# The line buffers of the first scan: four images side by side, or interleaved

## The chip, the cores and the metric

The kernel runs on one core of a Trainium2 chip. The core's engines each follow their own queue: TensorE (matmuls, with the weight loads beside them), VectorE, ScalarE, GpSimd and SyncE, which issues most DMAs; they meet at semaphores. The metric is the time of the whole kernel on the device, in microseconds (us). Three runs of the kernel before the change took 2135.49, 2137.81 and 2139.49 us, a median of 2137.81.

## The reference

The input x has 4 images of 64 channels of 128 x 128 pixels, in float32. Two blocks follow, each with a spatial mixer and a mixture of experts. The second block's spatial mixer is the part that matters here: four passes over the normalised image, down, up, to the right and to the left. In each, a line of the image depends on the line before it, for all lines in turn:

```
def step(carry, xi):                       # carry: the line before, xi: this line
    y = xi + relu(conv1d(carry, w))        # 9 taps along the line, 64 -> 64 channels, pad 4
    return y, y
_, ys = scan(step, xs[0], xs[1:])
```

So each pass is a chain of 127 convolutions over one line of 128 pixels, for four images at once, and a line can't begin before the line before it is complete.

## The kernel before

The kernel runs its stages one after the other: the wavelet mixer of block 0 (`wavelet_mixer`), the choice of tokens for its experts (`expert_choice`), then `apply_and_first_scan`, the stage of the change, three further passes (`scan_pass`, lines L1150 to L1314) and the second mixture (`top2_mixture`).

*How a line lies in memory.* A line of 128 pixels and 64 channels is folded: the even and the odd pixels stand on two halves of the 128 partitions, so that a line of one image is 64 columns. The 9 taps become `ND = 5` matmuls with a 128 x 128 weight block each, which read the same 64 columns at the column offsets d = 0 to 4. All lines of all images lie in `X`, seen as `Xl` (L950) with the axes slot, image, row, column: one image takes 64 x 64 float32 words of a partition in a slot, and two consecutive lines are in the two slots.

*The line buffers.* `g.yh` and `g.yl` hold the line just computed, with a margin of two columns on both sides: 68 columns for each image (L1807). The convolution is done in a one-pass matmul type (float32r), and to keep float32's precision the line is split: `yh` is the line rounded to that type, `yl` what is left. The taps are split the same way into `Thi` and `Tlo`. `convolve(n)` (L999) runs 15 matmuls of 256 columns into one PSUM bank: five taps of Tlo on yh, five of Thi on yh, five of Thi on yl. It waits for `hi` before the first and for `lo` before the eleventh (L1001, L1006).

*VectorE's part of a line*, `scan_line(n)` (L1104): when the 15 matmuls are done (`conv`), L1115 computes relu(conv) + x and writes it to yh (semaphore `hi`); L1117 computes the same once more and writes it to X as the result, in float32 (`full`); L1101 subtracts yh from it and writes yl (`lo`). All three have 256 elements on 128 partitions. Line 0 is a copy (L1108).

*What else runs in the stage.* In the same loop, written out by hand, the chunks that the scan will read are prepared, in steps t of four lines (i = 0 to 3), two chunks a step. TensorE's order (L1040 to L1057): `convolve`, then for i = 0 the matmuls of `delta` (L1018), for i = 1 `centre` (L1028), for i = 2 `variance` (L1037, L1038), for i = 3 `variance` and `centre`. VectorE's order (L1132 to L1147): `scan_line`, then for i = 0 and 1 `add_delta` (L1123), for i = 2 and 3 `norm` (L1129), which waits for ScalarE's rstd. ScalarE squares the centred chunk (L1066, L1068) and makes rstd (L1072, L1074), GpSimd splits the squares (L1092), SyncE loads the chunks and stores them. The scan stays `BEHIND = 11` lines behind, and its last lines have nothing beside them but the turning of the next pass's taps (L643, L652).

*Other lines that the prediction reads.* L773 and L778 are reductions in `expert_choice`: L773 over consecutive words, L778 over the same number of elements with 64 words from one to the next. L561 in `wavelet_mixer` reads and writes every second word. L1255 copies the first line of a pass to its buffer; in the second of the three later passes, at 1085 us, that line is a column of the image, with 64 words from one element to the next. L1350 copies a block of 128 consecutive words. L1208 is the convolution of the later passes.

Of the kernel before, what the change touches and what calls it, by code (L numbers as in the profile page):

```python
# [22 lines left out]
F32 = mybir.dt.float32  # L23
F32R = mybir.dt.float32r
# [3 lines left out]
ALU = mybir.AluOpType  # L28
AXX = mybir.AxisListType.X

P = 128
B, C, H, W = 4, 64, 128, 128
# [896 lines left out]
def apply_and_first_scan(nc, g, a):  # L929
# [6 lines left out]
    with ExitStack() as ctx:  # L936
# [7 lines left out]
        ps = [m.ps(f"ps{r}") for r in range(2)]  # L944
        xin, x2_out = g.xin, m.sems("x2o", B)
        s = {n: m.sem(n) for n in ("delta", "x2", "centred", "squared", "var", "lnv", "rstd", "normed")}
# [3 lines left out]
        Xl = g.X[:].rearrange("p (s b j w) -> p s b j w", s=2, b=B, j=HP)  # L950
# [3 lines left out]
        inner = slice(2, 2 + 64)  # L954
# [24 lines left out]
        with nc.Block() as block:  # L979
# [16 lines left out]

            @block.tensor
            def _(pe):
                def convolve(n):  # L999
                    out = ps[n % 2][:, 0:B * 64].rearrange("p (b w) -> p b w", b=B)  # L1000
                    pe.wait_ge(s["hi"], n)  # L1001
                    for t in (g.Tlo, g.Thi):
                        for d in range(ND):
                            pe.matmul(out, t[:, d * P:d * P + P], g.yh[:, :, d:d + 64],  # L1004
                                      start=(t is g.Tlo and d == 0), stop=False)
                    pe.wait_ge(s["lo"], n)  # L1006
                    for d in range(ND):
                        last = pe.matmul(out, g.Thi[:, d * P:d * P + P], g.yl[:, :, d:d + 64],  # L1008
                                         start=False, stop=(d == ND - 1))
                    last.then_inc(s["conv"], 1)  # L1010

                def delta(n):
                    k, p = divmod(n // 2, 2)
                    at = p * (TOK + PAD) + k * N
                    wait(pe, s["x2"], n)
                    wait(pe, s["lnv"], n - 1)
                    for i in range(2):
                        last = pe.matmul(dl[i][:], g.D[i * C:i * C + C, p], g.E[i * C:i * C + C, at:at + N],  # L1018
                                         start=True, stop=True)
                    last.then_inc(s["delta"], 2)  # L1020

                def centre(n):
                    wait(pe, s["x2"], n + 1)
                    wait(pe, s["normed"], n - 1)
                    src = buf(n).rearrange("p (q v) -> p v q", v=2)
                    for h, v in ((0, 0), (1, 1), (0, 1), (1, 0)):
                        rows = slice(h * C, h * C + C)
                        last = pe.matmul(xc[n % 2][v * C:v * C + C, h], g.Cm[rows, rows], src[rows, v],  # L1028
                                         start=True, stop=True)
                    last.then_inc(s["centred"], 1)  # L1030

                def variance(n):
                    wait(pe, s["parts"], n + 1)
                    wait(pe, s["high"], n + 1)
                    wait(pe, s["lnv"], n)
                    wait(pe, s["x2"], min(n // 2 * 2 + (4 if n % 2 else 2), CHUNKS))
                    pe.matmul(vv[:], Jr[:], sq_hi[n % 2][:], start=True, stop=False)  # L1037
                    pe.matmul(vv[:], Jr[:], sq_lo[n % 2][:], start=False, stop=True).then_inc(s["var"], 1)  # L1038

                for t in range(STEPS):  # L1040
                    for i in range(4):
                        n = line(t, i)
                        if n is not None and n >= 1:
                            convolve(n)
                        if i == 0 and t < PAIRS:
                            delta(2 * t)
                        if i == 1 and t < PAIRS:
                            centre(2 * t)
                        if i == 2 and 1 <= t <= PAIRS:
                            variance(2 * t - 1)  # L1050
                        if i == 3 and t < PAIRS:
                            variance(2 * t)
                            centre(2 * t + 1)
                        if n == FREE:
                            pe.wait_ge(s["normed"], CHUNKS - 1)
                            pe.wait_ge(g.unit_ready, 1)
                            turn_taps(pe, g, 1, wn, unit, banks[0])  # L1057
# [37 lines left out]
            @block.vector  # L1095
            def _(dve):
                def split(x, n):

                    wait(dve, s["full"], n)
                    dve.wait_ge(s["hi"], n + 1)  # L1100
                    dve.tensor_tensor(g.yl[:, :, inner], x, g.yh[:, :, inner].bitcast(F32), ALU.subtract  # L1101
                                      ).then_inc(s["lo"], 1)

                def scan_line(n):  # L1104
                    x = Xl[:, n % 2, :, n // 2:n // 2 + 1, :].rearrange("p b j w -> p b (j w)")
                    if n == 0:
                        wait(dve, s["normed"], B)
                        dve.tensor_copy(g.yh[:, :, inner], x).then_inc(s["hi"], 1)  # L1108
                        split(x, 0)
                        return  # L1110
                    conv = ps[n % 2][:, 0:B * 64].rearrange("p (b w) -> p b w", b=B)
                    dve.wait_ge(s["conv"], n)
                    if n % (2 * JR) == 0:
                        wait(dve, s["normed"], (n // (2 * JR) + 1) * B)
                    dve.scalar_tensor_tensor(g.yh[:, :, inner], conv, 0.0, x, ALU.max, ALU.add  # L1115
                                             ).then_inc(s["hi"], 1)
                    dve.scalar_tensor_tensor(x, conv, 0.0, x, ALU.max, ALU.add).then_inc(s["full"], 1)  # L1117
                    split(x, n)

                def add_delta(n):  # L1120
                    dve.wait_ge(s["delta"], n + 1)
                    dve.wait_ge(xin[n % B], n // B * 16 + 16)
                    dve.tensor_tensor(buf(n), dl[n % 2][:], buf(n), ALU.add).then_inc(s["x2"], 1)  # L1123

                def norm(n):
                    k, b = divmod(n, B)
                    at = b * HP * WP + k * (JR * WP)
                    dve.wait_ge(s["rstd"], n + 1)
                    dve.tensor_tensor(Xv[:, :, at:at + JR * WP], xc[n % 2], halves(sq(n)), ALU.mult  # L1129
                                      ).then_inc(s["normed"], 1)  # L1130

                for t in range(STEPS):  # L1132
                    for i in range(4):
                        n = line(t, i)
                        if n is not None:
                            scan_line(n)
                            if n == FREE - 4:
                                dve.wait_ge(s["delta"], CHUNKS - 2)
                                dve.tensor_tensor(unit, g.Cm[0:C, 0:C], g.J[0:C, 0:C], ALU.add).then_inc(g.unit_ready, 1)
                            if FREE + 3 <= n < FREE + 7:  # L1140
                                copy_taps(dve, g, 1, banks[0], n - FREE - 3)
                        if i < 2 and t < PAIRS:
                            add_delta(2 * t + i)
                        if i == 2 and 1 <= t <= PAIRS:
                            norm(2 * t - 1)
                        if i == 3 and t < PAIRS:
                            norm(2 * t)  # L1147
# [614 lines left out]
def metaformer_kernel(nc, a, out):  # L1762
    g = Shared()
    with ExitStack() as ctx:
# [30 lines left out]
        with ExitStack() as early:  # L1795
            me = Mem(nc, early, "g")
            g.E = me.sb("E", [P, 2 * TOK + PAD])
            g.T = {}
            with ExitStack() as choice:
                mc = Mem(nc, choice, "g")  # L1800
                g.cand = mc.right("cand", [P, B // 2, NG * K0])
                choice_constants(g)
                setup_block0(nc, g, a)
                wavelet_mixer(nc, g, a)
                g.D = me.sb("D", [P, B // 2, P])
                g.Thi, g.Tlo = me.sb("Thi", [P, ND * P], F32R), me.sb("Tlo", [P, ND * P], F32R)
                g.yh, g.yl = me.sb("yh", [P, B, 68], F32R), me.sb("yl", [P, B, 68], F32R)  # L1807
                expert_choice(nc, g, a)
            second = ctx.enter_context(ExitStack())
            g.T[1] = Mem(nc, second, "g").right("T1", [P, ND * P])  # L1810
            apply_and_first_scan(nc, g, a)
# [38 lines left out]
```

## Time and profile before

| | |
|---|---|
| Median of 3 runs | 2137.81 us (2135.49 to 2139.49) |
| Profiled execution | span 2135.2 us, 40582 instructions; the page gives no other time for it |
| TensorE busy | 2023.2 us (95%) |
| VectorE busy | 1193.0 us (56%) |
| First scan's convolutions | 1905 matmuls, 429.4 to 791.5 us |
| L1004 on Tlo, mean of one | 306 ns, 635 of them |
| L1004 on Thi, mean of one | 285 ns, 635 |
| L1008, mean of one | 288 ns, 635 |
| L1115, mean of one | 426 ns, 127 |
| L1101, mean of one | 449 ns, 128 |

The span runs from the first to the last instruction of one profiled execution. A busy TensorE isn't TensorE at its peak: its matmuls overlap, and a matmul's duration holds the filling and emptying of the array, so what one costs in a row is the step from its start to the next one's. The granted clock is the share of full speed that TensorE was given.

### The profile page before, as it was taken

The page shows a single profiled execution, that of the slowest core. Times are in us where ns is not written, and L with a number is a line of the kernel's source. Part 1 is how long each engine was busy: PE and PEld are TensorE (multiplying, and loading weights), DVE is VectorE, ACT ScalarE, POOL GpSimd, SP SyncE. Part 2 cuts the span into 40 slices and gives each one's busy share as a digit, 9 for nine tenths or more (in the row PEclk, how much of TensorE's full clock was granted, in tenths as well). Part 3 has the DMA queues.
Part 4 walks back from the last instruction along what each step waited for, and adds up shares of the span by engine and source line. Part 5 has one row for each costly group of instructions (what it writes and reads, how often), then busy time and mean ns, then how long its engine had stood idle before and what let it go on. Part 6 is the DMA issues. An engine that isn't in the chain of part 4 may idle for free. (4 is left out here: it accounts for less than half of the span.)

```text
span 2135.2 us, 40582 instructions
## 1 busy us (share of the span) xinstructions
PE 2023.2 (95%) x14414; PEld 1528.4 (72%) x14414; DVE 1193.0 (56%) x2548; ACT 1005.2 (47%) x2815; POOL 511.6 (24%) x622
## 2 busy tenths in 40 slices
PE   6999992699999989999999999999999799999998
PEld 3555551377777779999999999999999444444443
DVE  5777778666666653222222222232222599999998
ACT  4666664334444423333344444444444545455452
POOL 4555543222222210000000000000000554555541
PEclk9999996599999999999999999999999799999999
DMA  4955541223223210000000000000000466655653
GB/s 117 242 164 169 163 144 50 68 87 99 90 90 99 86 36 1 0 0 0 0 4 0 0 0 0 20 0 0 0 0 0 114 153 149 153 151 149 153 137 90
DMA packets 192672, 159.04 MB, mean 74 GB/s; under 512 B 25848, under 2 KB 159000, under 8 KB 192536
## 3 DMA queue, kind: packets, MB, share of 16 engines
q1 hardware_dynamic: 190840, 156.89, 26.4%
q8 instruction: 61, 1.00, 0.2%
q0 software_dynamic: 512, 0.53, 0.1%
q14 instruction: 75, 0.61, 0.1%
q10 hardware_dynamic: 1184, 0.00, 0.0%
HBM read 56.70 MB, written 67.11 MB: 58 GB/s over the span
## 5 line engine op out<-in xcount | busy, mean ns | idle before, releaser
L1208 PE MATMUL s_ps<-g_ring,g_T 128*128 128x128 f32 x7620 | 855.7, 274 | 8.5 <-DVE g_ring L1255 8.5
L1208 PEld LDWEIGHTS s_ps<-g_ring,g_T 128*128 128x128 f32 x7620 | 854.6, 192 | 9.2 <-DVE g_ring L1255 9.1
L1244 DVE SCALAR_TENSOR_TENSOR g_ring<-s_ps,s_xs 128x128 f32<-128x128 f32 x508 | 148.7, 293 | 418.3 <-PE s_ps L1208 418.3
L1685 DVE TENSOR_TENSOR tm_Z<-tm_pg,tm_nd 128x1024 f32<-128x1024 f32 x256 | 301.9, 1211 | 22.9 <-PE tm_pg L1525 22.5
L1307 ACT ACTIVATE g_X<-g_ring 128x256 f32<-128x256 f32 x254 | 172.3, 678 | 296.0 <-DVE g_ring L1244 296.0
L1539 PE MATMUL tm_po<-tm_Z,g_wexp 128*64 128x512 f32 x1024 | 249.2, 608 | 0.0
L1291 ACT ACTIVATE g_X<-g_ring 64x256 f32 x256 | 106.9, 418 | 205.5 <-DVE g_ring L1244 203.3
L1244 DVE SCALAR_TENSOR_TENSOR g_ring<-s_ps,g_X 128x128 f32<-128x128 f32 x254 | 74.4, 293 | 210.6 <-PE s_ps L1208 210.6
L1621 POOL TENSOR_TENSOR g_X<-g_x,g_X 128x512 f32<-128x512 f32 x64 | 82.9, 1298 | 349.7 <-POOLq L1184 286.0
L1302 ACT ACTIVATE s_xs<-g_X 128x256 f32<-128x256 f32 x254 | 161.3, 636 | 0.6 <-PEq L1184 0.6
L1539 PEld LDWEIGHTS tm_po<-tm_Z,g_wexp 128*64 128x64 f32 x1024 | 62.5, 137 | 109.9 <-issue 108.1
L1330 POOL MEMSET g_zero<- 128x1 f32 x1 | 0.1, 98 | 578.2 <-POOLq L1184 578.2
L1598 ACT ACTIVATE tm_gT<-tm_bankB 64x512 fp32r<-64x512 f32 x64 | 37.8, 591 | 202.0 <-PE tm_bankB L1513 202.0
L1004 PEld LDWEIGHTS af_ps<-g_yh,g_Tlo 128*128 128x128 f32 x635 | 85.0, 190 | 66.8 <-DVE g_yh L1115 54.3
L533 POOL TENSOR_TENSOR wm_sql<-g_X,wm_sqh 128x512 fp32r<-128x512 f32 x64 | 89.1, 1393 | 132.9 <-DVE wm_sqh L568 131.6
L1004 PE MATMUL af_ps<-g_yh,g_Tlo 128*128 128x256 f32 x635 | 111.5, 306 | 5.9 <-DVE g_yh L1115 4.2
L1115 DVE SCALAR_TENSOR_TENSOR g_yh<-af_ps,g_X 128x256 fp32r<-128x256 f32 x127 | 54.1, 426 | 90.4 <-PE af_ps L1008 87.7
L1008 PE MATMUL af_ps<-g_yl,g_Thi 128*128 128x256 f32 x635 | 99.2, 288 | 0.0
L1004 PE MATMUL af_ps<-g_yh,g_Thi 128*128 128x256 f32 x635 | 98.0, 285 | 0.0
L1525 PE MATMUL tm_pg<-tm_gT,g_sel 32*128 32x512 f32 x512 | 96.2, 449 | 1.2 <-DVE tm_Z L1685 1.1
L1008 PEld LDWEIGHTS af_ps<-g_yl,g_Thi 128*128 128x128 f32 x635 | 86.6, 192 | 0.0
L1004 PEld LDWEIGHTS af_ps<-g_yh,g_Thi 128*128 128x128 f32 x635 | 86.1, 190 | 0.0
(273 smaller groups left out, 2887.7 us busy)
## 6 DMA issues: line engine op xcount, KB each, us to landing
tm_nd<-g_X SPq DMA_DIRECT2D x256, 128.0 KB, 2.4
g_X<-in_x SPq DMA_DIRECT2D x128, 128.0 KB, 2.9
x1s<-g_X SPq DMA_DIRECT2D x64, 256.0 KB, 2.1
x1tok<-g_X SPq DMA_DIRECT2D x64, 256.0 KB, 2.5
g_x<-x2s SPq DMA_DIRECT2D x64, 256.0 KB, 2.9
y<-tm_yo SPq DMA_DIRECT2D x128, 128.0 KB, 2.5
g_X<-x1s SPq DMA_DIRECT2D x32, 256.0 KB, 2.8
x2s<-g_X SPq DMA_DIRECT2D x32, 256.0 KB, 2.0
```

Source lines behind the costliest of these rows:

```text
L533: pool.tensor_tensor(sq_lo[:], sq[c % 2], sq_hi[:].bitcast(F32), ALU.subtract).then_inc(s["parts"], 1)
L1004: pe.matmul(out, t[:, d * P:d * P + P], g.yh[:, :, d:d + 64], start=(t is g.Tlo and d == 0), stop=False)
L1008: last = pe.matmul(out, g.Thi[:, d * P:d * P + P], g.yl[:, :, d:d + 64], start=False, stop=(d == ND - 1))
L1208: last = pe.matmul(out, g.T[i][:, d * P:d * P + P], g.ring[(u - 1) % RING][:, images(c), d:d + 64], start=(d == 0), stop=(d == ND - 1))
L1244: dve.scalar_tensor_tensor(g.ring[n % RING][:, images(c), inner], conv, 0.0, x[:, images(c)], ALU.max, ALU.add).then_inc(y_ready[c], 1)
L1291: last = act.activation(dst.rearrange("p b j w -> p b (j w)"), src, ACT.Copy)
L1302: act.activation(xs[n % RING][:], line(*place(n)), ACT.Copy).then_inc(staged, 1)
L1307: act.activation(line(*place(n)), g.ring[n % RING][:, :, inner], ACT.Copy).then_inc(stored, 1)
L1525: last = pe.matmul(pg[q % 2][:, h * N:h * N + N], sel[rows, at:at + 2].rearrange("p e c -> p (e c)"), gT[i][rows], start=True, stop=True)
L1539: last = pe.matmul(po[i][h * C:h * C + C, :], wexp[:, ep], Z[q % 4][:, h], start=False, stop=(ep == EP - 1), skip_group_check=True)
L1621: pool.tensor_tensor(xv, natural(x2[t % 2][i][:]), xv, ALU.add).then_inc(s["x3"], 1)
L1685: dve.tensor_tensor(Z[q % 4][:], pg[q % 2][:].rearrange("p (h n) -> p h n", h=2), nd[t % 2][i][:], ALU.mult).then_inc(s["z"], 1)
```

## The change

The two buffers get the shape 68 columns by 4 images, instead of 4 images by 68 columns: in a partition the four images' words of one column stand beside each other. The window of a tap, `y[:, d:d + 64, :]`, is then one run of 256 words, where it was four runs of 64 with 68 words from the start of one to that of the next. The columns of the PSUM bank come in the same order, column by column, and VectorE's three operations follow it: they walk `x`, which keeps its place in X, across the images first. So x's elements are taken from four places in turn, one image's 64 x 64 words apart. Number and size of the instructions, semaphores and their waits, and all other stages are unchanged.

```diff
             def _(pe):
+                def window(y, d):
+
+                    return y[:, d:d + 64, :].rearrange("p w b -> p (w b)")
+
                 def convolve(n):
-                    out = ps[n % 2][:, 0:B * 64].rearrange("p (b w) -> p b w", b=B)
+                    out = ps[n % 2][:, 0:B * 64]
                     pe.wait_ge(s["hi"], n)
                     for t in (g.Tlo, g.Thi):
                         for d in range(ND):
-                            pe.matmul(out, t[:, d * P:d * P + P], g.yh[:, :, d:d + 64],
+                            pe.matmul(out, t[:, d * P:d * P + P], window(g.yh, d),
                                       start=(t is g.Tlo and d == 0), stop=False)
                     pe.wait_ge(s["lo"], n)
                     for d in range(ND):
-                        last = pe.matmul(out, g.Thi[:, d * P:d * P + P], g.yl[:, :, d:d + 64],
+                        last = pe.matmul(out, g.Thi[:, d * P:d * P + P], window(g.yl, d),
                                          start=False, stop=(d == ND - 1))
...
-                    dve.tensor_tensor(g.yl[:, :, inner], x, g.yh[:, :, inner].bitcast(F32), ALU.subtract
+                    dve.tensor_tensor(g.yl[:, inner, :], x, g.yh[:, inner, :].bitcast(F32), ALU.subtract
                                       ).then_inc(s["lo"], 1)
...
-                    x = Xl[:, n % 2, :, n // 2:n // 2 + 1, :].rearrange("p b j w -> p b (j w)")
+                    x = Xl[:, n % 2, :, n // 2, :].rearrange("p b w -> p w b")
...
-                        dve.tensor_copy(g.yh[:, :, inner], x).then_inc(s["hi"], 1)
+                        dve.tensor_copy(g.yh[:, inner, :], x).then_inc(s["hi"], 1)
...
-                    conv = ps[n % 2][:, 0:B * 64].rearrange("p (b w) -> p b w", b=B)
+                    conv = ps[n % 2][:, 0:B * 64].rearrange("p (w b) -> p w b", b=B)
...
-                    dve.scalar_tensor_tensor(g.yh[:, :, inner], conv, 0.0, x, ALU.max, ALU.add
+                    dve.scalar_tensor_tensor(g.yh[:, inner, :], conv, 0.0, x, ALU.max, ALU.add
                                              ).then_inc(s["hi"], 1)
                     dve.scalar_tensor_tensor(x, conv, 0.0, x, ALU.max, ALU.add).then_inc(s["full"], 1)
...
-                g.yh, g.yl = me.sb("yh", [P, B, 68], F32R), me.sb("yl", [P, B, 68], F32R)
+                g.yh, g.yl = me.sb("yh", [P, 68, B], F32R), me.sb("yl", [P, 68, B], F32R)
```

## Rows read from the trace of the kernel before

**Rows 1.** Windows: window, length, then busy time (instructions) of each engine, clock, DMA.

```profile
465.50:751.30 285.80, 284.39 (x2105) 218.49 (x2101) 185.42 (x401) 117.47 (x201) 64.10 (x50) 1.00 0.29 93
```

**Rows 2.** Timeline, one turn of four lines: start, duration, engine, line, operation, idle before.

```profile
602.69 0.88 PE L1004 MATMUL af_ps<-g_yh,g_Tlo 128*128 128x256 f32 x5
...
604.83 0.43 DVE L1115 SCALAR_TENSOR_TENSOR g_yh<-af_ps,g_X 128x256 fp32r<-128x256 f32 x1 [0.56 <-PE af_ps L1008]
...
605.78 0.88 PE L1004 MATMUL af_ps<-g_yh,g_Tlo 128*128 128x256 f32 x5
606.07 0.68 DVE L1123 TENSOR_TENSOR g_E<-af_dl,g_E 128x512 f32<-128x512 f32 x1
...
607.81 0.68 PE L1028 MATMUL af_xc<-g_E,g_Cm 64*64 64x256 f32 x8
607.92 0.43 DVE L1115 SCALAR_TENSOR_TENSOR g_yh<-af_ps,g_X 128x256 fp32r<-128x256 f32 x1 [1.17 <-PE af_ps L1008]
...
608.42 0.87 PE L1004 MATMUL af_ps<-g_yh,g_Tlo 128*128 128x256 f32 x5
...
608.71 0.43 DVE L1101 TENSOR_TENSOR g_yl<-g_X,g_yh 128x256 fp32r<-128x256 f32 x1
...
609.62 0.68 PEld L1008 LDWEIGHTS af_ps<-g_yl,g_Thi 128*128 128x128 f32 x5
...
609.73 0.78 PE L1008 MATMUL af_ps<-g_yl,g_Thi 128*128 128x256 f32 x5
...
610.35 0.39 PE L1037 MATMUL af_dl<-af_sqh,g_J 128*128 128x512 f32 x1
...
611.03 0.87 PE L1004 MATMUL af_ps<-g_yh,g_Tlo 128*128 128x256 f32 x5
...
612.39 0.69 DVE L1129 TENSOR_TENSOR g_X<-af_xc,g_E 128x512 f32<-128x512 f32 x1 [0.63 <-ACT g_E L1074]
...
614.13 0.88 PE L1004 MATMUL af_ps<-g_yh,g_Tlo 128*128 128x256 f32 x5
```

**Rows 3.** Timeline of the stage's tail, one weight load of a line.

```profile
778.99 0.67 PEld L1004 LDWEIGHTS af_ps<-g_yh,g_Tlo 128*128 128x128 f32 x5 [0.72 <-DVE g_yh L1115]
```

**Rows 4.** Source lines, one line's Thi and yl matmuls: duration min/median/max, first and last start.

```profile
L1004 PE MATMUL af_ps<-g_yh,g_Thi x2: 283/284/286, 603.4 to 603.5; 128*128 128x256 f32 x2
...
L1004 PE MATMUL af_ps<-g_yh,g_Thi x2: 284/287/290, 603.6 to 603.8; 128*128 128x256 f32 x2
...
L1004 PE MATMUL af_ps<-g_yh,g_Thi x1: 277/277/277, 603.9 to 603.9; 128*128 128x256 f32 x1
...
L1008 PE MATMUL af_ps<-g_yl,g_Thi x1: 282/282/282, 604.0 to 604.0; 128*128 128x256 f32 x1
...
L1008 PE MATMUL af_ps<-g_yl,g_Thi x2: 292/292/292, 604.1 to 604.3; 128*128 128x256 f32 x2
...
L1008 PE MATMUL af_ps<-g_yl,g_Thi x2: 279/284/289, 604.4 to 604.5; 128*128 128x256 f32 x2
```

**Rows 5.** Source line of the variance matmul; timeline of TensorE in a later pass.

```profile
L1037 PE MATMUL af_dl<-af_sqh,g_J x64: 390/390/797, 410.1 to 770.5; 128*128 128x512 f32 x64
...
899.76 6.41 PE L1208 MATMUL s_ps<-g_ring,g_T 128*128 128x128 f32 x56
```

**Rows 6.** Source line L1115, whole stage.

```profile
L1115 DVE SCALAR_TENSOR_TENSOR g_yh<-af_ps,g_X x127: 424/426/426, 433.0 to 791.5; 128x256 fp32r<-128x256 f32 x127
```

**Rows 7.** Source lines of other VectorE operations, in order or hopping.

```profile
L773 DVE TENSOR_REDUCE g_X<-g_X x1: 1221/1221/1221, 373.7 to 373.7; 128x16 f32<-128x1024 f32 x1
...
L778 DVE TENSOR_REDUCE g_X<-g_X x1: 1872/1872/1872, 377.2 to 377.2; 128x128 f32<-128x1024 f32 x1
...
L561 DVE SCALAR_TENSOR_TENSOR g_X<-wm_rec,g_b2c,g_X x128: 473/482/490, 28.9 to 327.6; 128x256 f32<-128x256 f32 x128
...
L1255 DVE COPY g_ring<-g_X x2: 339/340/342, 1085.2 to 1085.5; 128x128 f32<-128x128 f32 x2
...
L1350 DVE COPY g_rx<-g_Cm x1: 217/217/217, 1394.4 to 1394.4; 128x128 f32<-128x128 f32 x1
```

## The prediction

> **What bounds the kernel now.** I read the windows by stage first, then the timeline of one turn of the four-step loop, then the tail of the stage, and last the single instructions. The change touches only the stage of the first scan. Between 465.5 and 751.3 us TensorE is busy for 284.4 of 285.8 us at a granted clock of 1.00, its upper level of 2.4 GHz, and VectorE for 185.4 [rows 1]. TensorE's busy time holds pipeline tails, so the timeline has to say what ends last. In it four lines start at 602.69, 605.78, 608.42 and 611.03 and the next turn at 614.13: 3.09, 2.64, 2.61 and 3.10 us, 11.44 us a turn, and so over the whole stage [rows 2]. There are two kinds of gap between lines:
>
> - *Serial.* Line 608.42 starts when its g_yh is there: L1115 starts at 607.92, takes 426 ns, and the convolution follows within 0.1 us [rows 2, 6]. There a line is convolution, L1115, convolution, and the centre or variance matmuls between are shorter than the gap. The gaps behind the second and the third line of a turn are such (29 turns, 58 gaps); in the tail, where TensorE has nothing else and waits 0.72 us for g_yh, there are 9 more [rows 3]: 67.
> - *Covered.* L1115 of line 605.78 starts at 604.83 and ends at 605.26, but TensorE is still at its delta matmuls until the line starts at 605.78. L1115 has 0.47 us to spare here, if the 0.05 that a serial gap also needs is taken off [rows 2]. The gap behind the fourth line (variance, then centre) is like it: 59 in all.
>
> **Part 1: the columns of a tap (a gain).** A line is 15 matmuls, five taps for each of Tlo and Thi on yh and Thi on yl. The five yl matmuls from 609.73 to 610.35 take 124 ns a step [rows 2] and last 282, 292, 292, 289 and 279 ns, 287 in the mean [rows 4]: a step is the duration less 163. The Thi group lasts 283 and 286, then 284 and 290, then 277. So the middle taps are the slow ones. The diff fits this: today a tap's window starts 4 bytes after the last one's, in four runs of 64 columns, so only the first and the last tap start at a multiple of 16 bytes of the row; after it every window is one run and starts at such a multiple. The trace has one contiguous stream of this type, the variance matmul, 390 ns for 512 columns [rows 5]; against 277 for 256 that is 0.44 ns a column, 113 for 256, and 113 is also the step of a matmul that lasts 277. So I take 277 for all. The excess is 35 ns in Thi, 49 in yl, and 29 in Tlo (taken like Thi's last four, since its first only fills the pipeline): 113 ns a line. TensorE is on the path in both kinds of gap, so 127 x 113 = **14.4 us less**. Bounds: nothing (the columns are not what costs), and the 112 ns at which a weight load of this shape and a matmul alternate in the later passes (56 in 6.41 us, [rows 5]), 14 steps x 2.4 more: 147 ns a line, 18.7 us.
>
> **Part 2: VectorE's three operations a line (a loss).** L1115, L1117 and L1101 keep their 256 elements, but walk x across the images, so each element of x lies 16 KB (one image's 64 x 64 words) from the one before. L1115 and L1101 read one such stream; L1117 reads it and writes it. The trace has no such hop. The nearest rows [rows 7]: a reduction of 1024 elements takes 1221 ns in order and 1872 with hops of 64 words, 0.64 ns an element, 163 for 256; an operation on every second word (L561) takes 482 against L1115's 426, 56 more; a copy of 128 elements with hops of 64 words takes 340 against 217 in order, 123 more, 245 for 256, though a plain copy may lose more by it than these do. I take 163, the row with the long hopping stream and nothing else; 56 and 245 are the ends. A gain is excluded: no element is saved.
>
> The Trainium skill, "Vector Engine (DVE) Microarchitecture Reference", section 5.2 (measured stream behaviour on trn2), speaks against this change: a port keeps its rate only on runs of two or more adjacent words, and one source that hops at every element costs 1.73 instead of 1.054 ns a column. By it the loss would be 173 ns an operation and the sum 0.7 us higher. This trace's 0.64 ns an element agrees.
>
> On the path: L1115 counts in each serial gap, 67 x 163 = **10.9 us more**. In the 59 covered gaps it lies beside the matmuls, within the 0.47; without that cover it would cost 9.6. L1117 and L1101 lie beside the ten yh matmuls: L1101 ends at 609.14, and the first yl weights load at 609.62, 0.48 us later [rows 2]. The ten yh matmuls get 0.06 shorter, which leaves 0.42. L1101 takes 0.16 of it, L1117 between 0.16 (read and write hop together) and 0.33 (they add up); by the middle the two take 0.41 and are just hidden. Beyond that, each ns late costs 67 serial gaps one. At the end of the stage all three hold up the next: **0.6 us more**.
>
> Queued behind them on VectorE: L1123, which ends at 606.75 and would end 0.57 later, still before the centre matmuls at 607.81 that wait for it [rows 2]. The normalisation L1129 waits for ScalarE until 612.39; L1101 before it, 0.72 us after its line's start as in line 608.42, would end at 612.32. A turn holds 7.4 us of VectorE's work (185.4 of 285.8, [rows 1]) and gains 2.3, of 11.4: it is not the bound as a whole. L1108 runs once, off the path.
>
> **Sum.** -14.4 + 10.9 + 0.6 = -2.9 us. The profiled execution's span is 2135.2 us, 0.3 under the fastest of the three runs and 2.6 under their median, so its durations hold for the median to about a thousandth. 2137.8 - 2.9 = **2134.9 us**.
>
> **The rivals.**
>
> *B, the matmuls gain more.* One run in place of four brings the step to the later passes' 112 ns: 18.7 us instead of 14.4, 2130.6. For it: the four runs go, and not only their offsets. Against: the contiguous 512 columns need 0.44 ns each. The Trainium skill, "TensorE: Matmul & The Clock Gate", section "Back-to-back issue gap", gives N/2.4 + 2.5, 109 ns for 256 columns; by that rule the gain would be some 23 us and the time 2126. The trace's contiguous matmul, 390 ns for 512, speaks against it.
>
> *C, the hop is almost free.* Each image's words are still read in order, four streams in turn, and a hop costs no more than L561's 56 ns: 3.8 us in place of 10.9, 0.2 at the end, 2127.4. For it: L561. Against: the reduction's hops cost three times that. Section 5.2 of the Trainium skill's page on the Vector Engine also reports one stream between two regions 16 KiB apart at the full read rate; no run here shows it.
>
> *D, it doesn't do what it says.* The spread among taps comes from something else, such as the weight loads beside them, and the steps stay: only the loss is left, +11.5, 2149.3. For it: yl's taps last up to 292, Thi's up to 290, and the second is 292 in one and 286 in the other at the same offset. Against: first and last are quick in both.
>
> *E, slower: the low parts come late.* Place: the wait before the first yl matmul; the other yl matmuls and so the next L1115 stand behind it. It decides once L1117 and L1101 lose over 0.42 us together. At 0.2 an operation, double for L1117, they lose 0.6: 67 x 0.18 = 12.1, and L1115 costs 13.4, 0.8 at the end: 2149.7. At 245 and double: 67 x 0.315 = 21.1 and 16.4 and 1.0: 2161.9. For it: the forecast lies at the edge of the room, and L1117 hops on two ports. Against: at 163 and double it is only 0.07 a gap, 4.7 us.
>
> **How the numbers follow.** About 0.2%, 4.3 us, is what a measurement can tell from no change. The forecast has 0.42; 20 ns an operation and 25 ns a line either way, and that 4.7, give it 2130 to 2142, a third of it faster and the rest within. B has 0.14 and C 0.12, both faster; D has 0.08, slower; E has 0.24, 0.04 of it within. Faster 0.40, same 0.32, slower 0.28. The range goes down to where B and C hold together (18.7 less, 3.8 and 0.2 more), 2123, and up past D and E's first price, 2156.
>
> **What would show it.** Part 1: af_ps matmuls all at about 277 ns; if they keep 282 to 292, D. Part 2: L1115 and L1101 at about 590 ns, L1117 between 580 and 740; under 500 is C, over 625 E. The chain: serial lines of 2.66 to 2.69 us, covered ones of 2.98; a wait of TensorE for g_yl is E. The prediction is wrong if a line's time leaves these by over 0.1 us, or if the centre or variance matmuls begin to wait for VectorE.

## The result, and the profile after

The change makes the kernel slower: 2143.04 us (median of 9 runs, 2141.47 to 2145.46) against 2135.49 of the kernel before (9 runs, 2134.58 to 2139.52), a ratio of 1.0032 with a 95% interval of 1.0023 to 1.0041. The forecast was 2134.9, 2.9 us faster than the median then known; the range from 2123 to 2156 holds the result, but the sign is wrong.

| | before | after |
|---|---|---|
| Profiled span | 2135.2 us | 2143.6 us |
| yl matmul, median | 289 ns | 280 ns |
| Operation on the path (L1115, now L1119), median | 426 ns | 604 ns |
| Start of the first to start of the last low-part operation (L1101, now L1105) | 428.1 to 792.3, 364.2 us | 429.8 to 799.6, 369.8 us |

Three source lines of the kernel before, from which the table and the differences below are taken (duration ns min/median/max, first and last start):

```profile
L1008 PE MATMUL af_ps<-g_yl,g_Thi x635: 276/289/416, 431.7 to 791.2; 128*128 128x256 f32 x159
...
L1117 DVE SCALAR_TENSOR_TENSOR g_X<-af_ps,g_X x127: 412/414/424, 433.3 to 791.9; 128x256 f32<-128x256 f32 x127
...
L1101 DVE TENSOR_TENSOR g_yl<-g_X,g_yh x128: 425/427/531, 428.1 to 792.3; 128x256 fp32r<-128x256 f32 x128
```

The line numbers behind the diff are four higher: L1004 and L1008 are now L1008 and L1012; L1101, L1115 and L1117 are L1105, L1119 and L1121. Now the single instructions, one source line each, which answer to [rows 4, 6]:

```profile
L1008 PE MATMUL af_ps<-g_yh,g_Tlo x635: 275/282/581, 430.9 to 796.9; 128*128 128x256 f32 x159
...
L1008 PE MATMUL af_ps<-g_yh,g_Thi x635: 276/281/415, 432.2 to 797.5; 128*128 128x256 f32 x159
...
L1012 PE MATMUL af_ps<-g_yl,g_Thi x635: 274/280/415, 433.2 to 798.1; 128*128 128x256 f32 x159
...
L1119 DVE SCALAR_TENSOR_TENSOR g_yh<-af_ps,g_X x127: 582/604/616, 434.5 to 798.4; 128x256 fp32r<-128x256 f32 x127
...
L1121 DVE SCALAR_TENSOR_TENSOR g_X<-af_ps,g_X x127: 585/605/621, 435.1 to 798.9; 128x256 f32<-128x256 f32 x127
...
L1105 DVE TENSOR_TENSOR g_yl<-g_X,g_yh x128: 587/629/642, 429.8 to 799.6; 128x256 fp32r<-128x256 f32 x128
```

Both halves of the change are in these rows. The groups of taps no longer differ: the median is 280 to 282 ns in all three, where taps 1 to 3 stood at up to 292. And each of VectorE's operations is longer by 178 to 202 ns. One turn of four lines, the timeline that answers to [rows 2]:

```profile
606.55 0.86 PE L1008 MATMUL af_ps<-g_yh,g_Tlo 128*128 128x256 f32 x5
...
609.57 0.86 PE L1008 MATMUL af_ps<-g_yh,g_Tlo 128*128 128x256 f32 x5
...
611.65 0.61 DVE L1119 SCALAR_TENSOR_TENSOR g_yh<-af_ps,g_X 128x256 fp32r<-128x256 f32 x1 [0.67 <-PE af_ps L1012]
...
612.32 0.86 PE L1008 MATMUL af_ps<-g_yh,g_Tlo 128*128 128x256 f32 x5
...
612.82 0.62 DVE L1105 TENSOR_TENSOR g_yl<-g_X,g_yh 128x256 fp32r<-128x256 f32 x1
...
613.50 0.66 PEld L1012 LDWEIGHTS af_ps<-g_yl,g_Thi 128*128 128x128 f32 x5
...
615.06 0.86 PE L1008 MATMUL af_ps<-g_yh,g_Tlo 128*128 128x256 f32 x5 [0.18 <-DVE g_yh L1119]
...
618.12 0.38 PE L1008 MATMUL af_ps<-g_yh,g_Tlo 128*128 128x256 f32 x1
```

The lines start at 606.55, 609.57, 612.32 and 615.06, the next turn at 618.12: 3.02, 2.75, 2.74 and 3.06 us, where they took 3.09, 2.64, 2.61 and 3.10. The covered gaps got 0.04 to 0.07 us shorter, the serial ones 0.11 to 0.13 longer. In a serial gap L1119 starts at 611.65, ends at 612.26, and the line starts at 612.32. L1105 of this line ends at 613.44, and the weights for yl load at 613.50, as soon behind it as the line starts behind L1119. So the load waits for the low part. In some lines one sees what it costs, as in this one of the tail:

```profile
777.84 0.64 DVE L1105 TENSOR_TENSOR g_yl<-g_X,g_yh 128x256 fp32r<-128x256 f32 x1
...
777.90 0.66 PEld L1008 LDWEIGHTS af_ps<-g_yh,g_Thi 128*128 128x128 f32 x5
...
778.53 0.65 PEld L1012 LDWEIGHTS af_ps<-g_yl,g_Thi 128*128 128x128 f32 x5
```

The low part ends at 778.48, the yl loads begin 0.05 us later, and the five loads before them took 0.63 us, where those of line 609.57, in a covered gap, take 0.60 (610.15 to 610.75). The single loads in the trace give the sum. In some 66 lines the first yl load starts 52 to 62 ns behind the low part's end, and in the others 325 ns or more. In the 66 it comes 134 ns behind the load before it in the mean, in the others 116: 18 ns late, 1.2 us in all. No wait is listed for it in the profile, since the load before it is still running. In the tail TensorE's wait for g_yh grows from 0.72 us [rows 3] to 0.88:

```profile
785.50 0.66 PEld L1008 LDWEIGHTS af_ps<-g_yh,g_Tlo 128*128 128x128 f32 x5 [0.88 <-DVE g_yh L1119]
```

The window of the stage's middle (busy time of each engine, clock, DMA) has TensorE at the upper clock, as [rows 1] had; VectorE is busy for 237.5 of 286.0 us, where it was for 185.4 of 285.8.

```profile
470.00:756.00 286.00, 279.60 (x2076) 213.10 (x2073) 237.52 (x396) 115.32 (x196) 63.69 (x50) 1.00 0.28 93
```

*Where the 8.5 us between the two spans lie.* The stage grew by 5.6 us. Another 1.7 us came before it: L778 starts at 378.8 and not 377.2, in code that is unchanged, and it does so in some kernels below and not in others (378.9 in the first experiment, 377.2 in the third), so it isn't the change's. The last 1.2 us lies behind the stage's end, 1.0 of it in the next pass. The two windows of 16 us there, before and after, each from shortly ahead of the last split:

```profile
790.00:806.00 16.00, 13.13 (x102) 12.93 (x101) 5.02 (x24) 3.34 (x8) 1.20 (x2) 0.89 0.14 38
```

```profile
796.00:812.00 16.00, 12.27 (x83) 12.07 (x84) 6.27 (x24) 1.71 (x5) 1.20 (x2) 0.79 0.14 38
```

The granted clock is 0.89 in the one and 0.79 in the other: after the break between the stages it was at its lower level for longer. This too varies from run to run: among the runs of the kernel before that were taken beside experiment 4, the mean granted clock is 0.969 to 0.973. The ratio's interval, 4.9 to 8.8 us, holds the stage's 5.6.

### The profile page after: what moved, and what is told of

It is laid out like the page before. It is cut to its first block and busy times, and to the rows that moved or that the text cites. A ratio compares the mean times of both kernels' runs of the same rounds, so it can differ in the third digit from the quotient of the medians.

```text
span 2143.6 us, 40582 instructions
## 1 busy us (share of the span) xinstructions
PE 2021.7 (94%) x14414; PEld 1524.4 (71%) x14414; DVE 1262.1 (59%) x2548; ACT 1006.5 (47%) x2815; POOL 511.8 (24%) x622
## 5 line engine op out<-in xcount | busy, mean ns | idle before, releaser
L1625 POOL TENSOR_TENSOR g_X<-g_x,g_X 128x512 f32<-128x512 f32 x64 | 83.0, 1299 | 349.6 <-POOLq L1188 286.0
L1008 PEld LDWEIGHTS af_ps<-g_yh,g_Tlo 128*128 128x128 f32 x635 | 83.5, 189 | 76.1 <-DVE g_yh L1119 75.3
L1008 PE MATMUL af_ps<-g_yh,g_Tlo 128*128 128x256 f32 x635 | 109.7, 303 | 13.1 <-DVE g_yh L1119 10.3
L1119 DVE SCALAR_TENSOR_TENSOR g_yh<-af_ps,g_X 128x256 fp32r<-128x256 f32 x127 | 76.5, 603 | 58.5 <-PE af_ps L1012 55.3
L1012 PE MATMUL af_ps<-g_yl,g_Thi 128*128 128x256 f32 x635 | 96.6, 282 | 0.0
L1008 PE MATMUL af_ps<-g_yh,g_Thi 128*128 128x256 f32 x635 | 96.4, 282 | 0.0
L1008 PEld LDWEIGHTS af_ps<-g_yh,g_Thi 128*128 128x128 f32 x635 | 85.1, 189 | 0.0
L538 POOL TENSOR_TENSOR wm_xl<-g_X,wm_xh 128x512 fp32r<-128x512 f32 x64 | 81.7, 1276 | 13.6 <-DVE wm_xh L555 13.6
```

The costliest lines, as they stand in the source:

```text
L1008: pe.matmul(out, t[:, d * P:d * P + P], window(g.yh, d), start=(t is g.Tlo and d == 0), stop=False)
L1012: last = pe.matmul(out, g.Thi[:, d * P:d * P + P], window(g.yl, d), start=False, stop=(d == ND - 1))
```

## The experiments

Their theories: the first is that the tidy windows were worth some 50 ns a line from the outset, because a matmul with its own weight load can't go much faster, and that the hop costs what it costs on the serial gaps; the main rival is that VectorE's hops took half of the matmuls' gain. Ratios are to the kernel before on the same chip; lengths of the stage are taken as in the table, from the rows of the low-part operation.

**1. The columns alone.** Interleaved buffers, but VectorE reads 256 consecutive words of X and writes its result to 256 others (four rows of one image each, in place of one row of four images).

```diff
-                    x = Xl[:, n % 2, :, n // 2, :].rearrange("p b w -> p w b")
+                    def flat(n, b):
...
+                        return Xl[:, n % 2, b, n // 8 * 4:n // 8 * 4 + 4, :].rearrange("p j w -> p (j w)").rearrange("p (w b) -> p w b", b=B)
...
+                    x, y = flat(n, 0), flat(n, 1)
...
-                    dve.scalar_tensor_tensor(x, conv, 0.0, x, ALU.max, ALU.add).then_inc(s["full"], 1)
...
+                    dve.scalar_tensor_tensor(y, conv, 0.0, x, ALU.max, ALU.add).then_inc(s["full"], 1)
+                    split(y, n)
```

> The interleaved buffers with none of VectorE's hops: its three operations read and write runs of 256 words of x (other rows than the reference's). Theory 1 (a matmul of 256 columns with its own weight load has a floor near 118 ns a step, so the tidy windows were never worth more than some 50 ns a line): the af_ps matmuls stay at 280 ns as in the changed kernel, serial lines are 2.56 to 2.59 us, the kernel 6 to 7 us faster than before (2129 if before is 2135.5). Rival (VectorE's hops take read bandwidth from the matmuls and ate half of the gain): the matmuls drop to 277 ns or less, steps of 114, and the kernel is 13 to 15 us faster than before.

Measured: 2128.25 us, ratio 0.9958 (0.9945 to 0.9972). The source lines:

```profile
L1008 PE MATMUL af_ps<-g_yh,g_Thi x635: 275/281/416, 432.3 to 785.3; 128*128 128x256 f32 x159
...
L1012 PE MATMUL af_ps<-g_yl,g_Thi x635: 274/280/416, 433.4 to 785.9; 128*128 128x256 f32 x159
...
L1123 DVE SCALAR_TENSOR_TENSOR g_yh<-af_ps,g_X x127: 424/425/426, 434.7 to 786.2; 128x256 fp32r<-128x256 f32 x127
...
L1105 DVE TENSOR_TENSOR g_yl<-g_X,g_yh x128: 424/426/595, 429.8 to 787.0; 128x256 fp32r<-128x256 f32 x128
```

And from its timeline, two lines' first matmuls with a serial gap between them:

```profile
604.04 0.86 PE L1008 MATMUL af_ps<-g_yh,g_Tlo 128*128 128x256 f32 x5
...
606.63 0.62 PE L1008 MATMUL af_ps<-g_yh,g_Tlo 128*128 128x256 f32 x3
```

Without any hop the matmuls still last 280 to 281 ns. So VectorE's hops didn't lengthen the matmuls of the changed kernel: the rival falls. The columns are worth 7.0 us of the stage (429.8 to 787.0, 357.2), half of the predicted 14.4. The serial line between 604.04 and 606.63 takes 2.59 us. The median fell by 9.0. The profile's 8.8 are the stage's 7.0, 1.7 more ahead of it, and 3.5 less behind it, where this run's clock didn't fall at a break (granted clock 1.00 from 787 to 803 us). So 7.0, and not 9.0, is the columns' share.

**2. The hop alone.** The old buffers and windows; x is walked across the images.

```diff
...
+                def line_of(y):
...
+                    return y[:, :, inner].rearrange("p a (c b) -> p a c b", b=B)
...
-                    x = Xl[:, n % 2, :, n // 2:n // 2 + 1, :].rearrange("p b j w -> p b (j w)")
+                    x = Xl[:, n % 2, :, n // 2, :].rearrange("p b (a c) -> p a c b", c=16)
...
-                    dve.scalar_tensor_tensor(g.yh[:, :, inner], conv, 0.0, x, ALU.max, ALU.add
+                    dve.scalar_tensor_tensor(line_of(g.yh), conv, 0.0, x, ALU.max, ALU.add
```

> The old buffers and windows, with only the hop across the images in VectorE's three reads and one write of x (the elements are wired wrongly within a line). Theory 1: the matmuls stay as before (282 to 292 by tap, a convolution of 2.10 us), L1115's 426 becomes about 600, serial lines grow by 0.18 us, covered ones by nothing: 67 x 0.178 = 12 us slower than before (2147). Rival (hops also slow the matmuls): convolutions over 2.12 us, 15 us slower or more.

Measured: 2150.84 us, ratio 1.0061 (1.0047 to 1.0074).

```profile
L1008 PE MATMUL af_ps<-g_yl,g_Thi x635: 276/289/415, 432.8 to 803.5; 128*128 128x256 f32 x159
...
L1119 DVE SCALAR_TENSOR_TENSOR g_yh<-af_ps,g_X x127: 584/606/615, 434.1 to 803.9; 128x256 fp32r<-128x256 f32 x127
...
L1101 DVE TENSOR_TENSOR g_yl<-g_X,g_yh x128: 587/622/637, 429.3 to 805.0; 128x256 fp32r<-128x256 f32 x128
```

The matmuls are those of before (yl median 289), L1119 takes 606, and the stage 375.7 us, 11.5 more. The two halves together, -7.0 and +11.5, make +4.5 of the +5.6 that the whole change costs in the stage. The 1.1 us that are left show up only where both halves meet: the quicker matmuls reach the yl taps sooner, and the hops make the low part later. From its first to its last start a line's convolution takes 1768 ns in the changed kernel and 1760 in experiment 1 (means from the traces), 1.0 us over 127 lines; most of this is the late low part of the section above. No run takes that wait alone away.

**3. The hop off the path.** The changed kernel, but L1119 (here L1120) adds consecutive words of a weight tile in place of x.

```diff
+                    other = g.Thi[:, 0:B * 64].bitcast(F32).rearrange("p (w b) -> p w b", b=B)
...
-                    dve.scalar_tensor_tensor(g.yh[:, inner, :], conv, 0.0, x, ALU.max, ALU.add
+                    dve.scalar_tensor_tensor(g.yh[:, inner, :], conv, 0.0, other, ALU.max, ALU.add
```

> The changed kernel, but the operation on the path (L1119) adds 256 consecutive words of another tile in place of x; the two beside the matmuls still hop. Theory 1: what lies beside the yh matmuls costs nothing, so this is as fast as the kernel without any hop, 6 to 7 us under before, with the low part still ready 0.1 us or more before TensorE wants it. Rival (the low parts come late, or the longer VectorE queue holds up others): 3 us or more slower than the kernel without hops.

Measured: 2131.92 us, ratio 0.9976 (0.9966 to 0.9986).

```profile
L1120 DVE SCALAR_TENSOR_TENSOR g_yh<-af_ps,g_Thi x127: 424/425/426, 433.0 to 784.8; 128x256 fp32r<-128x256 f32 x127
...
L1122 DVE SCALAR_TENSOR_TENSOR g_X<-af_ps,g_X x127: 581/606/615, 433.3 to 785.1; 128x256 f32<-128x256 f32 x127
...
L1105 DVE TENSOR_TENSOR g_yl<-g_X,g_yh x128: 590/627/642, 428.2 to 785.7; 128x256 fp32r<-128x256 f32 x128
```

The two operations beside the matmuls hop for 606 and 627 ns, and the stage takes 357.5 us against 357.2 without any hop. What lies beside the yh matmuls is hidden all but for 0.3 us, so rival E of the prediction is no large term. (Here too the first yl load comes late, in 36 lines by 10 ns in the mean.) The medians differ by 3.7 us between these two kernels, with intervals that overlap; the profiles put no more than 0.3 of it into the stage.

**4. All taps at offset 0, old layout.** Four runs of 64 columns, each from a multiple of 16 bytes of its row.

```diff
-                            pe.matmul(out, t[:, d * P:d * P + P], g.yh[:, :, d:d + 64],
+                            pe.matmul(out, t[:, d * P:d * P + P], g.yh[:, :, 0:64],
...
-                        last = pe.matmul(out, g.Thi[:, d * P:d * P + P], g.yl[:, :, d:d + 64],
+                        last = pe.matmul(out, g.Thi[:, d * P:d * P + P], g.yl[:, :, 0:64],
```

> The kernel before with the windows of all five taps at column offset 0 (so the taps' shifts are left out): four runs of 64 columns, each starting on a multiple of 16 bytes. Theory 1 (the offset within 16 bytes made taps 1 to 3 slow, the number of runs costs nothing): all af_ps matmuls at 277 to 283 ns, a convolution near 2.04 us, about 6 us faster than before. Rival (it is the four runs, or the position of the tap in its group): durations keep spreading up to 292 by position, and the time stays within 2 us of before.

Measured: 2130.89 us, ratio 0.9972 (0.9961 to 0.9983).

```profile
L1004 PE MATMUL af_ps<-g_yh,g_Thi x635: 276/281/415, 432.0 to 784.3; 128*128 128x256 f32 x159
...
L1008 PE MATMUL af_ps<-g_yl,g_Thi x635: 277/283/291, 432.8 to 784.9; 128*128 128x256 f32 x159
...
L1101 DVE TENSOR_TENSOR g_yl<-g_X,g_yh x128: 425/427/578, 429.6 to 786.0; 128x256 fp32r<-128x256 f32 x128
```

With the four runs kept and only the offsets gone, the matmuls are as quick as in the new layout and the stage is as short as in experiment 1 (356.4 us against 357.2; in its first 6 us the granted clock was 0.79 here and 0.56 there, an estimate of 1.4 us at full speed, more than the difference). It was the offset, not the number of runs; one run in place of four gave nothing by itself. All five taps read the same columns here; the new layout's windows differ and are as quick, so that doesn't explain it.

**5. The new layout one word off.**

```diff
...
-                g.yh, g.yl = me.sb("yh", [P, 68, B], F32R), me.sb("yl", [P, 68, B], F32R)
+                g.yh_all, g.yl_all = me.sb("yh", [P, 68 * B + 4], F32R), me.sb("yl", [P, 68 * B + 4], F32R)
+                g.yh, g.yl = (t[:, 1:1 + 68 * B].rearrange("p (w b) -> p w b", b=B) for t in (g.yh_all, g.yl_all))
```

> The changed kernel with both line buffers moved by one word, so that every window is one run that starts 4 bytes after a multiple of 16. If a run that starts off costs a fixed bit per run, one run in place of four costs a quarter of it: matmuls at 280 to 283 ns, at most 2 us slower than the changed kernel (2143 to 2145). If the offset slows the whole stream, the matmuls go to 288 to 292 ns, a convolution is 2.10 us again, and the time is 6 us over the changed kernel (2149). VectorE's operations, now writing runs off by a word, may take a little more.

Measured: 2146.08 us, ratio 1.0040 (1.0026 to 1.0054), against 1.0032 for the changed kernel, each on its own chip: no difference that the intervals allow.

```profile
L1008 PE MATMUL af_ps<-g_yh,g_Thi x635: 277/283/416, 431.0 to 800.0; 128*128 128x256 f32 x159
...
L1012 PE MATMUL af_ps<-g_yl,g_Thi x635: 277/284/416, 432.1 to 800.6; 128*128 128x256 f32 x159
...
L1105 DVE TENSOR_TENSOR g_yl<-g_X,g_yh x128: 591/633/641, 428.7 to 802.0; 128x256 fp32r<-128x256 f32 x128
```

The medians are 283 and 284 where the changed kernel has 281 and 280, and the yl taps of the old layout up to 292; the stage takes 373.3 us, 3.5 more than in the changed kernel. One run that starts off costs less than four, but neither expectation's number is met cleanly.

**6. Half the columns.** 14 of 15 matmuls with 128 columns, so that half of each line's convolution is left out.

```diff
-                            pe.matmul(out, t[:, d * P:d * P + P], window(g.yh, d),
+                            cols = B * 64 if t is g.Tlo and d == 0 else 128
+                            pe.matmul(out[:, 0:cols], t[:, d * P:d * P + P], window(g.yh, d)[:, 0:cols],
...
```

> The changed kernel with 128 columns instead of 256 in 14 of the 15 matmuls of a line (half of each line's convolution is left out). If the weight load sets the step, steps stay at 107 to 118 ns and a convolution at 1.9 to 2.05 us, the time within 15 us of the changed kernel. If the stream of columns sets it, steps fall to some 60 ns and a convolution to 1.2 us: some 100 us less in the stage, unless VectorE's operations then take over as the bound (about 1.9 us a line), which caps the gain near 80 us.

Measured: 2386.47 us in one run, against 2137.34 of before. Neither expectation. A window in the stage, and one in the next pass of the same run:

```profile
470.00:790.00 320.00, 320.00 (x1385) 247.84 (x1385) 156.49 (x264) 75.70 (x131) 41.92 (x33) 0.50 0.17 55
...
1050.00:1290.00 240.00, 240.00 (x2145) 239.62 (x2144) 65.47 (x221) 88.53 (x212) 0.00 (x0) 1.00 0.00 0
```

In its timeline, the Thi and yl groups of one line:

```profile
600.84 1.27 PE L1009 MATMUL af_ps<-g_yh,g_Thi 128*128 128x128 f32 x5
601.91 1.27 PE L1013 MATMUL af_ps<-g_yl,g_Thi 128*128 128x128 f32 x5
```

The clock was at its lower level, 0.50, in this window, where TensorE never paused in the profile, and on to the stage's end at 1040 us. The number of columns alone is not the reason: the next pass has matmuls of 128 columns with their own weight loads too, and runs at 1.00, 2145 of them in 240 us or 112 ns each. What held the clock down in the stage stays open. The steps can still be read, beside the first line of the changed kernel, which also ran at the lower level:

```profile
432.18 1.27 PE L1008 MATMUL af_ps<-g_yh,g_Thi 128*128 128x256 f32 x5
433.24 1.27 PE L1012 MATMUL af_ps<-g_yl,g_Thi 128*128 128x256 f32 x5
```

Five matmuls take 1.07 us there with 128 columns and 1.06 with 256 (from the Thi row to the yl row). Half the columns save nothing at the same clock: the columns don't set a step of 213 ns, and what is left of the pair is the weight load.

**7. Three quarters of the columns.** The same with 192 for 128 (a quarter of the convolution is left out), to see the load at the upper clock.

> The changed kernel with 192 columns instead of 256 in 14 of the 15 matmuls of a line (a quarter of the line's convolution is left out). With 128 columns the clock stayed at its lower level and every step was 213 ns, the time of a weight load there; what the load allows at the upper level is still open. If the clock stays at 1.00 and the load sets the step, steps are 107 to 112 ns, 0.1 us a line less than with 256 columns. If instead a step is the columns plus some 11 ns, it is near 91 ns and a convolution some 0.37 us shorter. If the clock falls to 0.50 again, steps are 213 once more, and it stays open.

Measured: 2141.36 us in one run, before 2137.98. The middle of the stage ran at 1.00. The window there:

```profile
470.00:760.00 290.00, 284.75 (x2169) 216.09 (x2167) 247.40 (x415) 120.56 (x205) 65.80 (x52) 1.00 0.28 94
```

Two groups of weight loads of one line, from the timeline:

```profile
605.89 0.64 PEld L1009 LDWEIGHTS af_ps<-g_yh,g_Thi 128*128 128x128 f32 x5
606.45 0.64 PEld L1013 LDWEIGHTS af_ps<-g_yl,g_Thi 128*128 128x128 f32 x5
```

And the Thi matmuls of a few lines, by source line:

```profile
L1009 PE MATMUL af_ps<-g_yh,g_Thi x30: 272/274/280, 600.1 to 614.8; 128*128 128x192 f32 x30
```

Five pairs of load and matmul take 0.56 us, 112 ns a step, though 192 columns alone would take a quarter less than 256. So at the upper clock the step is 112 with 192 columns as with the 128 of [rows 5]: the load holds it there. With 256 columns that start well it is 118 (280 to 282 less the 163 of the prediction), and before it was 122 in the mean. The Trainium skill, "TensorE: Matmul & The Clock Gate", section "LDWEIGHTS (loading the stationary operand)", gives columns / 1.2, 107 ns for 128; these 112 lie 5 ns above it. The 109 of its section "Back-to-back issue gap", which the prediction's rival B took for these pairs, is given there for a matmul alone, and for a stream of load and matmul pairs the section says that both set the spacing; with 256 columns the step here stays at 118 in the mean.

The kernel as a whole gained little by it: the yh taps are now so quick that in some 62 lines the first yl load waits for the low part (179 ns behind the load before it, in the other lines 112), and from 760 to 800 us the granted clock was 0.73.

**8. The fetch ahead: a version that beats both.** The changed kernel, complete; ScalarE copies x of the next lines into four interleaved buffers, so that the operation on the path reads consecutive words. In each step of the loop the copy for the next step's line 0 stands ahead of ScalarE's second square, the others behind it. Every eighth line, whose chunk has only just been normalised, still hops.

```diff
+        xi = [m.sb(f"xi{r}", [P, 64, B]) for r in range(4)]
+        staged = m.sem("staged")
...
+                def fetch(t, i):
+                    n = line(t, i)
+                    if n is None or n % 8 == 0:
+                        return
+                    act.wait_ge(s["normed"], (n // 8 + 1) * B)
+                    wait(act, s["full"], n - 4)
+                    act.activation(xi[n % 4][:], across(n), ACT.Copy).then_inc(staged, 1)
...
+                    early = x if n % 8 == 0 else xi[n % 4][:]
+                    if n % 8:
+                        dve.wait_ge(staged, n - n // 8)
+                    dve.scalar_tensor_tensor(g.yh[:, inner, :], conv, 0.0, early, ALU.max, ALU.add
+                    dve.scalar_tensor_tensor(x, conv, 0.0, early, ALU.max, ALU.add).then_inc(s["full"], 1)
```

> The changed kernel with the whole computation: ScalarE copies each line's x into an interleaved buffer of its own a few lines ahead, so that the operation on the path reads consecutive words (every eighth line still hops). Theory 1: the hop leaves the path, the gain of the windows stays: 5 to 7 us faster than before (2129 to 2130.5), serial lines 2.57 us. Rival (ScalarE has no room, its rstd or the fetch itself comes late, or its hopping reads disturb the others): the on-path operation waits for the fetch or the normalisation comes late, and the time is at or above before's 2135.5.

Measured: 2131.45 us, ratio 0.9972 (0.9962 to 0.9983): about 6 us faster than the kernel before.

```profile
L1140 DVE SCALAR_TENSOR_TENSOR g_yh<-af_ps,af_xi x112: 424/425/426, 433.8 to 785.4; 128x256 fp32r<-128x256 f32 x112
L1140 DVE SCALAR_TENSOR_TENSOR g_yh<-af_ps,g_X x15: 584/608/615, 453.4 to 767.4; 128x256 fp32r<-128x256 f32 x15
...
L1092 ACT ACTIVATE af_xi<-g_X x112: 632/656/692, 431.3 to 776.2; 128x256 f32<-128x256 f32 x112
...
L1123 DVE TENSOR_TENSOR g_yl<-g_X,g_yh x128: 590/628/1121, 430.0 to 786.4; 128x256 fp32r<-128x256 f32 x128
```

The starts of three lines in its timeline, each by its first weight load:

```profile
602.99 0.65 PEld L1014 LDWEIGHTS af_ps<-g_yh,g_Tlo 128*128 128x128 f32 x5 [0.76 <-DVE g_yh L1140]
...
605.58 0.65 PEld L1014 LDWEIGHTS af_ps<-g_yh,g_Tlo 128*128 128x128 f32 x5 [0.40 <-DVE g_yh L1140]
...
608.13 0.41 PEld L1014 LDWEIGHTS af_ps<-g_yh,g_Tlo 128*128 128x128 f32 x3 [0.43 <-DVE g_yh L1140]
```

The operation on the path is back at 425 ns for 112 lines, and lasts 608 for the 15 that hop; ScalarE's copies take 656 each, beside all else. The two serial lines take 2.59 and 2.55 us, and the stage 356.4, about as without any hop (357.2 in experiment 1, whose clock rose some 3 us later in the stage).

## Why the prediction was wrong

*The step that failed is Part 1's size.* "14.4 us less": the columns alone gave 7.0. The mechanism held: taps 1 to 3 were slow because of where their windows started (experiment 4), and the change made all alike. But "So I take 277 for all" took the quickest tap for the common one, though the other aligned tap, d = 0, stood in the same rows with 283 and 282 [rows 4]. It was backed by "0.44 ns a column, 113 for 256", a slope between one 256-column and one 512-column matmul, which read the 390 ns as a price per column. In truth the matmuls settled at 280 to 282, a step of 118, with the weight load's 112 close under it. The saving is 55 ns a line (7.0 us over 127 lines) and not 113, about 4 ns a step and not 8. Of the 8.5 us between the stage's +5.6 and the forecast's -2.9, 7.4 are this term. The bound that I did write down, the 112 of the later passes, was a floor set by the load; I used it as the far end of a gain and not as a reason to expect little.

*Part 2 held.* 163 ns was taken, 178 measured for L1119: 67 x 0.178 = 11.9 us instead of 10.9, and the hop alone cost 11.5 in the stage. Section 5.2 of the Trainium skill's "Vector Engine (DVE) Microarchitecture Reference" gives 1.73 instead of 1.054 ns a column, an estimate of 173 for 256, and the 178 is near it. L1117 lost 191 and not twice the 163, so a hop on reading and writing together cost hardly more than on reading alone. L1101 lost 202.

*The path held.* 67 serial gaps, 59 covered: serial lines grew, covered ones shrank. With the measured stages of experiments 1 and 2 in place of my terms the sum is -7.0 + 11.5 = +4.5 us, against 5.6 in the stage.

*The cover was a little short.* The prediction had the two operations just hidden, in a room of 0.42 us. That room left out the 0.05 that a release takes, which the prediction had counted at the covered gaps; with it the room is 0.37, and L1117 and L1101 lost 0.191 + 0.202 = 0.39. So the first yl load came some 18 ns late in 66 lines, 1.2 us in all, and most of the 1.1 that the sum lacks is probably there. No matmul of centre or variance began to wait for VectorE.

*The rivals.* B and C fell: a step of about 118 at 256 columns and not 112, no hop under 178 ns. E came true, but in the size of about 1 us and not of its prices. D was the nearest to the truth of those on the slower side, with 2149.3, though not in mechanism: half of the gain was missing, not all of it. What stays open is why a step with 256 columns is 118 and not the 112 of the load, and why one run a word off (experiment 5) costs as much as it did.

## What to carry to other kernels

Before a matmul's operand is laid out anew, look at how far its step lies above that of its weight load: at most that distance is to be had, and here it was less than half of it (55 of the prediction's 147 ns a line). A new layout has a price where the data is written and read, and the price counts by place: the same 180 to 200 ns a line cost 11.5 us on the operation that the next line waits for, and about 1 us on the two beside the matmuls. So move the hop to where there is cover, here to an idle engine ahead of time, and keep the gain.

## What the runs showed of the hardware that I had not expected

A float32r matmul of 256 columns in four runs lasted 281 to 283 ns in the median when its runs start on a multiple of 16 bytes of the row (experiment 4), and 284 to 292 when they start 4, 8 or 12 bytes off [rows 4]. One run in place of four made no difference where they start well (280 to 282), but a smaller loss where they start off (283 and 284, experiment 5). A VectorE operation whose operand changes among four streams 16 KB apart at each element takes 0.70 ns an element more (604 against 426 for 256); each of the four streams by itself is read in order, and that didn't help here. And in the one run with 128 columns in 14 of 15 matmuls, back to back with their weight loads, TensorE was granted 0.50 to the stage's end, where the runs with 192 and 256 columns got 1.00 in its middle: leaving out half of the work made the kernel 249 us slower. Matmuls of 128 columns with their weight loads ran at 1.00 in the next pass of the same run, so their size by itself doesn't hold the clock down.
